# Query projection of a fused cross-attention kernel: by batch, or turned for teams of three batches

## Chip, cores, metric

One core of a Trainium2 chip. The time is device microseconds of one execution. The kernel is one launch with five engines (PE for products, DVE, ACT, POOL, and SP, which here only issues DMAs), each with its own instruction list in a fixed order; they meet by semaphores.

## What is computed

For each of 16 batches (100 query rows, 361 context rows, width 512, float32): grouped-query attention with 32 query heads, 8 key/value heads of width 16, an output projection with residual and layer norm, and then a second, single-headed cross-attention with residual. Cut to what matters:

```
q = x @ Wq + bq;  k = c @ Wk + bk;  v = c @ Wv + bv
scores = einsum('bkgld,bksd->bkgls', q, k) / sqrt(16) + mask
attn = softmax(scores);  out = einsum('bkgls,bksd->bkgld', attn, v)
x = layernorm(out @ Wo + bo + x) * gamma + beta
s = (x @ w_q.T) @ (c @ w_k.T).T / sqrt(512)
x = x + alpha * ((softmax(s) @ (c @ w_v.T)) @ w_o.T)
```

## The kernel before

Precision is kept by splitting a float32 operand into a high and a low part (`_h`, `_l`); `product` (L707 to L711) then runs three matmuls for one. All four lists are written out by hand, call by call: batch b's `heads`, batch b-1's `scores` and `values`, and batch b-2's later stages are interleaved in pieces on PE.

- Query projection, per batch b: `x_turned_in` loads x transposed (xT, one buffer); ACT `x_high` and POOL `x_low` split it; PE `q_part` runs 4 x 3 matmuls with x as the weights (100 columns) and Wq moving (512 columns) into `work` bank 1; DVE `q_natural` adds the bias (`row_n`); PE `turn_q` transposes in four pieces; ACT `q_high` and DVE `q_low` split, with the scale 0.25; SP `queries_out` writes both parts to DRAM (`q_dr`) in two DMAs. `k_part` and `v_part` (Wk, Wv as 128-column weights, context moving, 362 columns) and `turn_v` use the same bank.
- `stacks_in` reads keys and queries back as stacked operands `ks`, `qs`. PE `heads` (L750) computes each head's scores in natural layout only for the row maximum, which DVE `maxima` takes (L2372). `turn_maxima`, `maxima_high`, `maxima_low` turn and split 16 maxima for each half of the heads; SP `maxima_in` (L246) copies them as two more rows into `qs`. `scores` waits for both (`m_in`), once for each half.
- `scores` (L730, L737, L738) computes transposed scores minus maximum; DVE and ACT move them to SBUF, POOL and DVE add the mask, ACT takes exp. `values` (L766) multiplies with V and a ones column; the rest (`y_part`, `xm_part`, `s1_part`, `cx_part`, `d_part`, L823 and L874) finishes layer norm and the second attention.
- At the start, `fold_m` (L883) and `fold_n` (L897) multiply pairs of second-layer weights once; weights are split by `high_part` and `low_part`; POOL clears and sets rows of `ks` and `qs` (`zero_rows`, `one_rows`).

Of the kernel before, what the change touches and what calls it, by code (L numbers as in the profile page):

```python
# [5 lines left out]
F32 = mybir.dt.float32  # L6
# [8 lines left out]
P = 128  # L15
# [4 lines left out]
JL = J * L  # L20
END = B - 1
# [20 lines left out]

def ring(b, par, dmas=1):

    return (8 * b - 8 * par + 16) * dmas


def build(nc, xT_d, x_d, ctxT_d, ctx_d, mask_d, maskT_d, wq_d, wk_d, wv_d, wo_d, bq_d, bk_d, bv_d,
          bo_d, gamma_d, beta_d, w1q_d, w1k_d, w1v_d, w1o_d, alpha_d, out_d):
    with ExitStack() as ctx:  # L50
# [19 lines left out]
        bq_b, gamma_b, beta_b, bo_b = (sb(n, [L, H]) for n in ("bq_b", "gamma_b", "beta_b", "bo_b"))  # L70
        bk_c, bv_c = sb("bk_c", [P, 1]), sb("bv_c", [P, 1])
# [7 lines left out]
        x_h, x_l = sb("x_h", [P, JL], F32R), sb("x_l", [P, JL], F32R)  # L79
        c_h, c_l = sb("c_h", [P, KT * SP2], F32R), sb("c_l", [P, KT * SP2], F32R)  # L80
        row_n = sb("row_n", [L, H])
        q_h, q_l = sb("q_h", [P, JL], F32R), sb("q_l", [P, JL], F32R)
# [9 lines left out]
        mt_h = [sb(f"mt_h{h}", [NH // 2, L], F32R) for h in range(2)]  # L92
        mt_l = [sb(f"mt_l{h}", [NH // 2, L], F32R) for h in range(2)]
# [26 lines left out]

        def turned_of(b):
            return r_b if b == END else turned

        def parts(b):
            return (x_h, x_l) if b == END else (u_h, u_l)


        k_dr = nc.dram_tensor("k_dr", (2, 2, HD, KVH, SC * P), F32, kind="Internal").ap()
        q_dr = nc.dram_tensor("q_dr", (2, 2, HD, KVH, JL), F32, kind="Internal").ap()
# [13 lines left out]
        q_mm, q_nat, q_tr, qh_ok, ql_ok = (sem(n) for n in ("q_mm", "q_nat", "q_tr", "qh_ok", "ql_ok"))  # L143
# [30 lines left out]
        def _(sp):  # L174
# [11 lines left out]
            def biases():  # L186
                sp.dma_start(bk_c[:, :], bk_d).then_inc(w_b, 16)
                sp.dma_start(bv_c[:, :], bv_d).then_inc(w_b, 16)
                sp.dma_start(bq_b[:, :], bq_d).then_inc(w_b, 16)
# [15 lines left out]
            def fold_n_in(k):  # L205
                if k == 0:
                    sp.wait_ge(wh_ok["q"], 1)
                    sp.wait_ge(wl_ok["q"], 1)
# [16 lines left out]
            def stacks_in(b, half, r0, r1):  # L225
                p = b % 2
                if r0 == 0:
                    wait(sp, q_out, 32 * (b + 1))
# [4 lines left out]
                for r in range(r0, r1):  # L233
# [3 lines left out]
                             q_dr[p, :, :, gs, :].rearrange("r d g c -> (r d) g c")).then_inc(st_in[half][p], 16)  # L237

            def maxima_in(b, half):
# [3 lines left out]
                for row, t in ((TERMS, mt_h[half]), (TERMS + 1, mt_l[half])):  # L243
# [70 lines left out]
            def queries_out(b):  # L314
                p = b % 2
                wait(sp, qh_ok, b + 1)
                wait(sp, ql_ok, b + 1)
                wait(sp, st_in[0][p], 96 * (b // 2))
                wait(sp, st_in[1][p], 96 * (b // 2))
                sp.dma_start(q_dr[p, 0, :, :, :].rearrange("d g c -> g d c"), q_h[:, :].bitcast(F32)).then_inc(q_out, 16)  # L320
                sp.dma_start(q_dr[p, 1, :, :, :].rearrange("d g c -> g d c"), q_l[:, :].bitcast(F32)).then_inc(q_out, 16)
# [17 lines left out]

            weights_q()  # L340
            x_turned_in(0)
            ctx_turned_in(0)
            fold_m_in(0)
            weights_k()
            biases()
            weights_o()
            weights_v()
            fold_m_in(1)
            fold_n_in(0)
            fold_n_in(1)  # L350
            x_turned_in(1)
            queries_out(0)
            keys_out(0)
# [4 lines left out]
            ctx_turned_in(1)  # L358
            stacks_in(0, 1, 0, 2)
            queries_out(1)  # L360
            mask_turned_in(0)
            stacks_in(0, 1, 2, 4)
            mask_in(1)
            fold_m_in(3)
            x_turned_in(2)
# [4 lines left out]
            stacks_in(1, 0, 2, 4)  # L370
            x_turned_in(3)
            norm_in()
            ctx_in(0)
            residual_in(0)
            maxima_in(0, 1)
            stacks_in(1, 1, 0, 2)
            stacks_in(1, 1, 2, 4)
            queries_out(2)
            ctx_turned_in(3)
            mask_turned_in(1)  # L380
            keys_out(2)
            mask_in(2)
            rows_out(0, 0)
            maxima_in(1, 0)
            stacks_in(2, 0, 0, 2)
            stacks_in(2, 0, 2, 4)
            rows_out(0, 1)
            stacks_in(2, 1, 0, 2)
            sums_in(0)
            rows_in(0)  # L390
            maxima_in(1, 1)
            x_turned_in(4)
            reciprocals_out(0)
            stacks_in(2, 1, 2, 4)
            reciprocals_in(0)
            queries_out(3)
            ctx_turned_in(4)
            keys_out(3)
            maxima_in(2, 0)
            mask_in(3)  # L400
            mask_turned_in(2)
            rows_out(1, 0)
            stacks_in(3, 0, 0, 2)
            stacks_in(3, 0, 2, 4)
            late_keys_in(0)
            rows_out(1, 1)
            stacks_in(3, 1, 0, 2)
            mask_turned_in(3)
            sums_in(1)
            maxima_in(2, 1)  # L410
            stacks_in(3, 1, 2, 4)
            rows_in(1)
            x_turned_in(5)
            reciprocals_out(1)
            late_keys_in(1)
            reciprocals_in(1)
            residual_in(1)
            rows_out(2, 0)
            ctx_in(1)
            mask_in(4)  # L420
            queries_out(4)
            maxima_in(3, 0)
            keys_out(4)
            stacks_in(4, 0, 0, 2)
            stacks_in(4, 0, 2, 4)
            stacks_in(4, 1, 0, 2)
            rows_out(2, 1)
            maxima_in(3, 1)
            result_out(0)
            ctx_turned_in(5)  # L430
            residual_in(2)
            sums_in(2)
# [3 lines left out]
            x_turned_in(6)  # L436
            mask_turned_in(4)
            reciprocals_in(2)
            rows_out(3, 0)
            ctx_turned_in(6)  # L440
            queries_out(5)
            mask_in(5)
# [3824 lines left out]
```

## Time and profile before

| | us |
|---|---|
| median of 3 runs | 670.9 (666.88 to 673.54) |
| the profiled execution | 673.24 |
| its span, first to last instruction | 671.5 |
| PE busy in the span | 637.4 |
| DVE, POOL, ACT busy | 494.7, 398.4, 395.9 |
| mean granted TensorE clock | 0.992 |

The span is what all views divide; the execution's own time is 1.74 us longer. A matmul's listed duration includes its way through the array, which overlaps with the next one, so what a matmul costs is the distance between two starts.

### The profile page before, as it was taken

Reading aid. Unit: us, or ns where it says so; the run is one execution under the profiler, and the core shown is the slowest. Engines: PE = TensorE matmul, PEld = TensorE weight load, DVE = VectorE, ACT = ScalarE, POOL = GpSimd, SP = SyncE. Lnnn points to the kernel's source line nnn. Section 1 sums busy time; section 2 is a strip of 40 time slices with the busy share of each in tenths; the row PEclk is TensorE's granted clock in tenths of the full one; section 3 lists DMA queues with packets and bytes.
Section 4 is the critical chain, followed back from the end, with each engine's and each line's share of the span. In section 5 each row is a group of like instructions: output and inputs, shape, how many; then the busy total and the mean of one; then the engine's idle time right before and its main releaser. Section 6 shows DMA issues by size and latency. Waiting matters only on the chain.

```text
span 671.5 us, 11779 instructions
## 1 busy us (share of the span) xinstructions
PE 637.4 (95%) x3720; PEld 467.3 (70%) x3720; DVE 494.7 (74%) x1453; ACT 395.9 (59%) x588; POOL 398.4 (59%) x254
## 2 busy tenths in 40 slices
PE   3989889999999999999999999999999999999887
PEld 2646557777767878777777778787777777766454
DVE  2258678877688787878787887878787888885742
ACT  3314576666657666666656576666667666666321
POOL 7243758756475766667665657666676666563220
PEclk9999888999999999999999999999999999999999
DMA  8687755755574766757475757667675755534212
GB/s 287 217 180 206 163 158 140 195 162 139 141 252 111 223 164 190 165 174 208 132 214 120 232 119 225 161 194 165 183 194 145 197 143 149 120 98 137 88 45 71
DMA packets 47354, 110.93 MB, mean 165 GB/s; under 512 B 10094, under 2 KB 31662, under 8 KB 46782
## 3 DMA queue, kind: packets, MB, share of 16 engines
q1 hardware_dynamic: 47294, 110.19, 60.0%
q8 instruction: 30, 0.49, 0.3%
q14 instruction: 30, 0.25, 0.1%
HBM read 87.29 MB, written 22.46 MB: 163 GB/s over the span
## 4 chain that ended last, share of the span: by engine, by line
PE 74%; DMA 9%; POOL 5%; issue 5%; DVE 2%; SPq 2%; ACT 2%; POOLq 0%; DVEq 0%; ACTq 0%
PE mx_ps L750 11%; PE work L709 10%; PE work L710 10%; PE work L711 10%; PE o_ps L766 8%; PE work L823 5%; PE work L874 5%; PE sc_ps L737 3%; DMA qs<-mt_l 3%; PE sc_ps L730 3%; PE sc_ps L738 3%; PE work L779 3%; POOL pr L3914 3%; DMA late<-r_dr 2%; DMA k_dr<-k_l 1%
## 5 line engine op out<-in xcount | busy, mean ns | idle before, releaser
L2372 DVE CUSTOM_DVE_ANT_0 mx_ps<-mx_ps,mask_n 100x361 f32<-100x361 f32 x512 | 271.4, 542 | 68.5 <-PE mx_ps L750 63.6
L3914 POOL TENSOR_TENSOR pr<-pr,mask_t 128x800 f32<-128x800 f32 x124 | 236.8, 1917 | 72.2 <-ACT pr L3218 69.8
L750 PE MATMUL mx_ps<-ks,qs 96*100 96x362 f32 x512 | 182.2, 370 | 3.3 <-DMA qs<-q_dr 2.3
L3225 ACT ACTIVATE pr<-pr 128x1200 f32<-128x1200 f32 x128 | 149.3, 1206 | 9.5 <-POOL pr L3914 5.6
L3218 ACT ACTIVATE pr<-sc_ps 128x800 f32<-128x800 f32 x124 | 104.0, 839 | 76.4 <-PE o_ps L766 50.3
L750 PEld LDWEIGHTS mx_ps<-ks,qs 96*100 96x100 f32 x512 | 84.4, 166 | 40.4 <-DVE mx L2372 12.2
L2358 DVE TENSOR_TENSOR pr<-sc_ps,mask_t 128x400 f32<-128x400 f32 x124 | 70.8, 571 | 26.0 <-PE sc_ps L730 14.4
L3926 POOL TENSOR_TENSOR c_l<-cT,c_h 128x1448 fp32r<-128x1448 f32 x16 | 53.3, 3330 | 55.1 <-ACT c_h L3250 55.1
L766 PE MATMUL o_ps<-pr,va 128*32 128x400 f32 (+1 forms) x768 | 73.9, 519 | 0.0
L2372 DVE DVE_READ_ACCUMULATOR2_ANT mx<- 100x1 f32 x512 | 72.0, 141 | 0.0
L823 PEld LDWEIGHTS work<-late 128*128 128x128 f32 (+1 forms) x384 | 49.7, 191 | 7.0 <-issue 5.9
L730 PE MATMUL sc_ps<-qs,ks 98*128 98x400 f32 x128 | 48.8, 381 | 4.2 <-DMA qs<-mt_l 4.0
L823 PE MATMUL work<-late 128*128 128x100 f32 (+1 forms) x384 | 52.2, 274 | 0.0
L874 PE MATMUL work<-late 128*100 128x362 f32 x128 | 49.1, 472 | 0.7 <-ACT late L3281 0.7
L737 PE MATMUL sc_ps<-qs,ks 98*128 98x400 f32 x128 | 47.0, 367 | 2.8 <-DMA qs<-mt_l 2.3
L766 PEld LDWEIGHTS o_ps<-pr,va 128*32 128x32 f32 (+1 forms) x768 | 22.3, 112 | 34.6 <-issue 32.2
L738 PE MATMUL sc_ps<-qs,ks 98*128 98x400 f32 x128 | 44.4, 347 | 0.0
L709 PE MATMUL work<-wq_h,x_h 128*100 128x512 f32 x64 | 30.5, 476 | 10.9 <-POOL x_l L3920 10.9
L3920 POOL TENSOR_TENSOR x_l<-xT,x_h 128x400 fp32r<-128x400 f32 x16 | 18.4, 1149 | 28.9 <-ACT x_h L3244 28.9
L730 PEld LDWEIGHTS sc_ps<-qs,ks 98*128 98x128 f32 x128 | 24.3, 190 | 12.2 <-DMA qs<-mt_l 4.7
L737 PEld LDWEIGHTS sc_ps<-qs,ks 98*128 98x128 f32 x128 | 24.4, 191 | 8.4 <-DMA qs<-mt_l 3.1
L3931 POOL TENSOR_SCALAR ve<-mv 100x1 f32<-100x1 f32 x16 | 7.5, 467 | 36.9 <-DVE mv L2453 36.9
(157 smaller groups left out, 1207.1 us busy)
## 6 DMA issues: line engine op xcount, KB each, us to landing
qs<-q_dr SPq DMA_DIRECT2D x64, 200.0 KB, 4.3
ks<-k_dr SPq DMA_DIRECT2D x128, 96.0 KB, 3.7
late<-in_ctx SPq DMA_DIRECT2D x16, 768.0 KB, 7.3
cT<-in_ctxT SPq DMA_DIRECT2D x16, 724.0 KB, 5.5
late<-in_ctxT SPq DMA_DIRECT2D x16, 724.0 KB, 6.0
o_dr<-o_s SPq DMA_DIRECT2D x30, 200.0 KB, 3.9
xT<-in_xT SPq DMA_DIRECT2D x16, 200.0 KB, 3.9
q_dr<-q_h SPq DMA_DIRECT2D x16, 200.0 KB
```

Of the source, the lines that this page charges most:

```text
L709: nc.tensor.matmul(dst, lh, rh, start=(k == 0), stop=False)
L730: nc.tensor.matmul(sc_ps[:, 0, 0:JL], ks[p][:, g, 0:P], qs[p][:, g, :], start=True, stop=True).then_inc(s0_mm, 1)
L737: nc.tensor.matmul(sc_ps[:, 1, 0:JL], ks[p][:, g, P:2 * P], qs[p][:, g, :], start=True, stop=True)
L750: nc.tensor.matmul(mx_ps[0:L, n % 2, 0:SP2], qs[p][0:TERMS, g, L * j:L * (j + 1)], ks[p][0:TERMS, g, 0:SP2], start=True, stop=True).then_i ...
L766: mm = nc.tensor.matmul(o_ps[32 * q:32 * (q + 1), 0:JL], va[p][0:k, c, 4 * half + q, :], pr[0:k, q, c, :], start=(c == 0), stop=(c == SC - 1))
L823: mm = nc.tensor.matmul(work[:, late_bank(b), L * t:L * (t + 1)], ctx_n[0:k, c, P * t:P * (t + 1)], p1_t[0:k, c, :], start=(c == 0), stop= ...
L874: mm = nc.tensor.matmul(work[0:L, late_bank(b), 0:SP2], turned_of(b)[:, L * k:L * (k + 1)], cT_s[:, SP2 * k:SP2 * (k + 1)], start=(k == 0) ...
L2358: V.tensor_tensor(pr[:, g % 4, 0, :].rearrange("p (j l) -> p j l", j=J), sc_ps[:, 0, 0:JL].rearrange("p (j l) -> p j l", j=J), mask_t[p][: ...
L2372: V.tensor_tensor_reduce(out=src, in0=src, in1=mask_n[p][:, :], scale=1.0, scalar=-3.0e38, op0=ALU.add, op1=ALU.max, accum_out=mx[p][:, n: ...
L3218: A.activation(pr[:, g % 4, 1:3, :], sc_ps[:, 1:3, 0:JL], ACT.Copy).then_inc(sc_cp, 1)
L3225: A.activation(t, t, ACT.Exp).then_inc(ex_ok, 1)
L3914: G.tensor_tensor(t, t, mask_t[p][:, 1:3, :].unsqueeze(2).to_broadcast([P, 2, J, L]), ALU.add).then_inc(sc_pool, 1)
```

## The change

From batch 4 on, queries are projected for three batches at once (batches 4 to 6, 7 to 9, 10 to 12, 13 to 15), and turned: Wq is the weights (128 columns, one of four blocks j), and x of three batches moves (300 columns). The result comes out transposed, so bias and split are one ACT and one DVE instruction for each j, and `q_natural` and `turn_q` go for these batches. The results go to DRAM by `team_out`: six DMAs for each j, of runs of 100 elements (400 bytes), where `queries_out` has two DMAs for each batch with runs of 400 elements. The scale 0.25 is folded into Wq and the bias.

Batch 0's projection is ordered by terms: products with the high halves first, by halves of Wq, whose split is now done in two pieces. Matmuls whose result nobody reads are put into PE's list: 24 of 128x128 float32 before the first product, and 49 of 512 columns in the first batches: 5 before the first heads (`fill_first`), 19 in four groups right ahead of a batch's scores (`fill_scores`, three of them in batches 0 and 1, one in batch 4), and 25 in fifteen groups of 1 to 4 among the heads (`keep_busy`, each behind a wait on DVE's or ACT's reading of the bank that it writes). `mt_h` and `mt_l` become one pair of tiles for both halves, so a half's `maxima_high` waits until the other half's DMAs have landed. All five lists are reordered; x is the first load, `keys_out(0)` moves ahead of `x_turned_in(1)` and `queries_out(0)`, and POOL's `x_low(0)` and `c_low(0)` move ahead of `zero_rows(0)`.

```
+ALONE = 4
+TEAMS = ((4, 3), (7, 3), (10, 3), (13, 3))
+def sent(t, j):
+    return 32 * (ALONE + J * sum(n for _, n in TEAMS[:t]) + (j * TEAMS[t][1] if j else 0))
...
+            def team_out(t, j):
+                b0, n = TEAMS[t]
+                wait(sp, qh_ok, ALONE + J * t + j + 1)
+                wait(sp, ql_ok, ALONE + J * t + j + 1)
+                for k in range(n):
+                    for r, src in ((0, q_h), (1, q_l)):
+                        sp.dma_start(q_dr[b0 + k, r, :, :, j, :].rearrange("d g l -> g d l"),
+                                     src[:, L * k:L * (k + 1)].bitcast(F32)).then_inc(q_out, 16)
...
+            def team_part(t, j, k0, k1):
+                b0, n = TEAMS[t]
+                js = slice(P * j, P * (j + 1))
+                if j == 0 and k0 == 0:
+                    pe.wait_ge(xh_ok, b0 + n)
+                    pe.wait_ge(xl_ok, b0 + n)
+                if k0 == 0:
+                    bank(1, ql_ok, ALONE + J * t + j + 1)
+                for k in range(k0, k1):
+                    mm = product(work[:, 1, 0:n * L], wq_h[:, k, js], wq_l[:, k, js], xs_h[:, k, 0:n, :],
+                                 xs_l[:, k, 0:n, :], k, KT - 1)
...
+            def fill_scores(b, g, c, count):
+                pe.wait_ge(*((sc_add, 8 * b + g) if c == 0 else (sc_cp, 8 * b + g)))
+                for _ in range(count):
+                    nc.tensor.matmul(sc_ps[0:L, 2 if c else 0, :], wk_h[:, 0, 0:L], wq_h[:, 0, :], start=True, stop=True)
...
+            def keep_busy(count, free, value):
+                pe.wait_ge(free, value)
+                dst = sc_ps[0:L, 2, :] if free is fl_ok and value == 3 else o_ps[0:L, :]
+                for _ in range(count):
+                    nc.tensor.matmul(dst, wk_h[:, 0, 0:L], wq_h[:, 0, :], start=True, stop=True)
...
+            warm_up(24)
+            fold_m(3, 0, 1)
             q_part(0, 0, 4)
+            fold_m(1, 0, 1)
+            turn_q(0)
...
             def maxima_low(b, half):
                 dve.wait_ge(mh_ok[half], b + 1)
-                wait(dve, m_in[half], 32 * b)
+                wait(dve, m_in[1 - half], 32 * (b + half))
...
+            def team_low(t, j):
+                n = TEAMS[t][1] * L
+                dve.wait_ge(qh_ok, ALONE + J * t + j + 1)
+                dve.wait_ge(q_out, sent(t, j))
+                V.scalar_tensor_tensor(q_l[:, 0:n], work[:, 1, 0:n], bq_c[:, j:j + 1], q_h[:, 0:n].bitcast(F32),
+                                       ALU.add, ALU.subtract).then_inc(ql_ok, 1)
...
+            def team_high(t, j):
+                n = TEAMS[t][1] * L
...
+                act.wait_ge(q_mm, ALONE + J * t + j + 1)
+                act.wait_ge(q_out, sent(t, j))
+                A.activation(q_h[:, 0:n], work[:, 1, 0:n], ACT.Identity, bias=bq_c[:, j:j + 1]).then_inc(qh_ok, 1)
...
             constants()
-            zero_rows(0)
             x_low(0)
             c_low(0)
+            settle(cl_ok, 1)
+            zero_rows(0)
```

## Rows read from the trace of the kernel before

**Rows 1.** The page's part 1: busy us (share of the span) x instructions.
```profile
PE 637.4 (95%) x3720; PEld 467.3 (70%) x3720; DVE 494.7 (74%) x1453; ACT 395.9 (59%) x588; POOL 398.4 (59%) x254
```
**Rows 2.** Busy time of each engine in stretches: one middle batch, and the end.
```profile
272.49:309.25 36.76, 36.76 (x232) 28.36 (x236) 29.66 (x90) 24.30 (x36) 24.16 (x15) 1.00 0.66 177
...
600.00:640.00 40.00, 35.79 (x209) 21.53 (x202) 28.25 (x58) 19.07 (x29) 14.59 (x13) 1.00 0.33 108
640.00:671.50 31.50, 24.70 (x130) 16.50 (x128) 8.80 (x18) 6.29 (x17) 3.39 (x5) 0.99 0.20 62
```
**Rows 3.** The same view of early stretches: us, PE, PEld, DVE, ACT, POOL, clock, DMA, GB/s.
```profile
0.00:10.87 10.87, 0.00 (x1) 0.03 (x1) 2.29 (x2) 3.62 (x3) 8.97 (x11) 1.00 0.74 256
10.87:19.30 8.43, 8.34 (x23) 4.96 (x24) 1.96 (x3) 3.59 (x4) 3.32 (x1) 1.00 0.95 357
...
67.00:117.00 50.00, 44.11 (x237) 29.75 (x236) 36.64 (x123) 31.96 (x45) 34.76 (x19) 0.90 0.60 154
...
78.00:82.00 4.00, 4.00 (x28) 1.32 (x27) 1.57 (x5) 0.70 (x2) 0.17 (x1) 0.67 0.23 51
```
**Rows 4.** PE's instructions in order of time, in one middle batch.
```profile
286.38 0.39 PE L709 MATMUL work<-wq_h,x_h 128*100 128x512 f32 x1
286.61 0.40 PE L710 MATMUL work<-wq_l,x_h 128*100 128x512 f32 x1
...
293.47 0.39 PE L750 MATMUL mx_ps<-ks,qs 96*100 96x362 f32 x1
293.70 0.51 PE L779 MATMUL work<-ident,row_n 100*128 100x100 f32 x4
294.04 0.83 PE L823 MATMUL work<-late 128*128 128x100 f32 x6
...
296.88 0.33 PE L709 MATMUL work<-c_h,wk_h 128*128 128x362 f32 x1
297.05 0.33 PE L710 MATMUL work<-c_l,wk_h 128*128 128x362 f32 x1
```
**Rows 5.** The chain that ended last, in order of time, first 42 us: start, us, what.
```profile
0.73 4.89 DMA late<-in_wq
...
5.65 1.91 ACT wq_h L3185
...
8.14 2.64 POOL x_l L3920
...
12.44 0.43 PE work L709
...
19.98 2.30 DVE wo_l L2338
...
25.36 7.94 DMA k_dr<-k_l
...
35.58 5.57 DMA qs<-q_dr
```
**Rows 6.** The waits of PE: us in total, times, longest us.
```profile
PE sc_ps L730 <- DMA qs<-mt_l: 4.0, 2, 2.8
...
PE sc_ps L737 <- DMA qs<-mt_l: 2.3, 3, 1.4
```
**Rows 7.** A maxima DMA and the scores behind it, in order of time.
```profile
304.13 0.59 SPq L246 DMA_DIRECT2D qs<-mt_l  x1
...
308.22 0.35 PE L737 MATMUL sc_ps<-qs,ks 98*128 98x400 f32 x1
```
**Rows 8.** DMA issues by line: times, KB each, median us to landing.
```profile
qs<-mt_l SPq DMA_DIRECT2D x32, 6.2 KB, 2.4
```
**Rows 9.** L320's issues: SP's ns for one, min/median/max.
```profile
L320 SPq DMA_DIRECT2D q_dr<-q_h x16: 594/620/715, 23.3 to 555.3; - x16
```
**Rows 10.** The page's part 3: packets, MB, share of 16 engines' time.
```profile
q1 hardware_dynamic: 47294, 110.19, 60.0%
```
**Rows 11.** Groups of DVE instructions by line and shape.
```profile
L2401 DVE TENSOR_TENSOR row_n<-work,bq_b 100x512 f32<-100x512 f32 x16 | 11.0, 687 | 6.5 <-PE work L711 6.4
```

More of the change, by code:

```diff
@@ L91, in build @@
         mx = [sb(f"mx{p}", [L, NH]) for p in range(2)]
-        mt_h = [sb(f"mt_h{h}", [NH // 2, L], F32R) for h in range(2)]
-        mt_l = [sb(f"mt_l{h}", [NH // 2, L], F32R) for h in range(2)]
+        mt_h = sb("mt_h", [NH // 2, L], F32R)
+        mt_l = sb("mt_l", [NH // 2, L], F32R)
         mask_t = [sb(f"mask_t{p}", [P, SC, L]) for p in range(2)]
@@ L242, in maxima_in @@
                 wait(sp, ml_ok[half], b + 1)
-                for row, t in ((TERMS, mt_h[half]), (TERMS + 1, mt_l[half])):
+                for row, t in ((TERMS, mt_h), (TERMS + 1, mt_l)):
                     dst = qs[p][row:row + 1, 4 * half:4 * half + 4, :].bitcast(F32).rearrange(
@@ L771, in turn_maxima @@
                 p = b % 2
+                if b == 0 and half == 0:
+                    pe.wait_ge(zero_ok, 2)
                 pe.wait_ge(a_mx, NH * b + 16 * (half + 1))
@@ L951, in pack_rows, with fill_first @@
                                  start=(half == 0), stop=(half == 1)).then_inc(g_mm2[half], 1)
+            def fill_scores(b, g, c, count):
+                pe.wait_ge(*((sc_add, 8 * b + g) if c == 0 else (sc_cp, 8 * b + g)))
+                for _ in range(count):
+                    nc.tensor.matmul(sc_ps[0:L, 2 if c else 0, :], wk_h[:, 0, 0:L], wq_h[:, 0, :], start=True, stop=True)
+            def fill_first(count):
+                for _ in range(count):
+                    nc.tensor.matmul(mx_ps[0:L, 1, :], wk_h[:, 0, 0:L], wq_h[:, 0, :], start=True, stop=True)
@@ L1096, in _ @@
+            q_part(3, 3, 4)
+            heads(2, 3, 5)
+            fill_scores(1, 4, 1, 3)
             scores(1, 4, 1, 3)
             turn_q(3)
+            scores(1, 4, 0, 1)
+            heads(2, 5, 6)
+            values(1, 0)
+            heads(2, 6, 8)
+            k_part(3, 0, 1)
+            heads(2, 8, 9)
+            scores(1, 5, 1, 3)
             heads(2, 9, 10)
-            values(1, 0)
+            k_part(3, 1, 2)
             heads(2, 10, 12)
-            scores(1, 4, 0, 1)
-            k_part(3, 0, 1)
@@ L1436, in _ @@
+            scores(5, 4, 1, 3)
+            k_part(7, 0, 1)
+            heads(6, 12, 13)
             cx_part(3, 0, 1)
-            heads(6, 9, 10)
-            turn_q(7)
+            heads(6, 13, 14)
+            scores(5, 4, 0, 1)
             cx_part(3, 1, 2)
-            heads(6, 10, 11)
+            heads(6, 14, 15)
+            k_part(7, 1, 2)
+            scores(5, 5, 1, 3)
             cx_part(3, 2, 3)
-            heads(6, 11, 12)
+            scores(5, 5, 0, 1)
+            heads(6, 15, 16)
@@ L1693, in _ @@
-            q_part(10, 3, 4)
-            heads(9, 7, 9)
+            turn_v(9)
+            values(8, 0)
+            heads(9, 7, 8)
             turn_p1(6)
-            values(8, 0)
+            heads(9, 8, 9)
+            team_part(2, 3, 0, 1)
+            scores(8, 4, 0, 1)
+            heads(9, 9, 10)
+            scores(8, 4, 1, 3)
             cx_part(6, 0, 1)
-            heads(9, 9, 10)
-            turn_q(10)
+            heads(9, 10, 11)
             cx_part(6, 1, 2)
-            heads(9, 10, 11)
+            heads(9, 11, 12)
@@ L3088, in _ @@
             centre(12)
+            maxima(14, 22, 23)
             shift(12)
@@ L4011, in _ @@
             add_mask(3, 0)
-            x_low(5)
             add_mask(3, 1)
+            x_low(8)
+            c_low(5)
             add_mask(3, 2)
@@ L4131, in _ @@
             add_mask(11, 0)
-            x_low(13)
+            c_low(13)
             add_mask(11, 1)
```

2999 lines of the change are left out of this document (1499 added, 1500 removed).

## The prediction

> **What bounds the kernel now.** I read the page's shares first. PE is busy 95% of the span, the next engine 74% [rows 1], which leaves 671.5 - 637.4 = 34.1 us in which PE does nothing. That average hides stages, so the second view is the busy time by stretches. In a middle batch, which lasts 36.76 us, PE is busy for all of it, DVE for 29.66, ACT 24.30, POOL 24.16 [rows 2]: there a microsecond off PE is a microsecond off the time, until DVE becomes the limit. The last 71.5 us are different: PE is idle for 4.2 us up to 640 and for 6.8 after it [rows 2]. At the start PE waits 10.87 us for its first operands. Then it runs slowly: from 10.87 to 19.30 the starts of 512-column products stand 0.43 us apart [rows 5], against 0.23 later [rows 4], although the page prints a granted clock of 1.00 there [rows 3]; 0.43 us for 512 columns is 1.2 GHz, 0.23 is near 2.4. Between 67 and 117 us the mean granted clock is 0.90 and PE busy 44.11 of 50 [rows 3]. The waits of PE show what stops it: scores waiting for maxima DMAs, 4.0 and 2.3 us in five waits [rows 6]. The third view is the chain at the start [rows 5]: load of Wq, its split, POOL's x_l (2.64 us), slow products, then the split of Wo (which SP waits for before it may issue more), the keys' way to DRAM (7.94 us), the stacks' way back (5.57 us), and heads at 41.3.
>
> **Teams (batches 4 to 15).** I price a matmul by the distance of starts. With 512 columns it is 0.23 us, with 128-column weights and 362 columns 297.05 - 296.88 = 0.17 (0.165 over several) [rows 4]. Removed per batch: 12 x 0.23 = 2.76 us. `turn_q` holds PE from 293.70 to 294.04, and the head ahead of it takes 0.23 in place of 0.17 [rows 4]: 0.40 us together. That is 3.16 us. Added per team: 4 x 4 x 3 = 48 matmuls of 300 columns with 128-column weights, 16 per batch. No row has that form. The line through the two prices is (0.230 - 0.165)/150 = 0.43 ns a column, so 300 columns cost 0.165 - 62 x 0.00043 = 0.138; I take 0.141 for a slightly larger fixed part. From above it is bounded by 0.165, if weights of 128 columns can't follow each other faster than in those rows; from below by 300 columns at 2.4 GHz, 0.125. So 16 x 0.141 = 2.26 us (2.00 to 2.64). Gain 3.16 - 2.26 = 0.90 us a batch, 12 batches: **10.8 us** (6.2 to 13.9). PE must be the limit for all of this to be seen. A team lays 6.8 us on one batch and a half, and batches without a team have 36.8 - 3.2 = 33.6 us of PE work. DVE there loses `q_natural`, 0.69 us [rows 11], and its share of q_l, and is at some 28.4 us, 85% of 33.6: it still fits. The stage that falls short is the end: the removed `q_part(14)` and `q_part(15)` lie before 600 us, where PE is nearly full, so I count them whole, with 6.2 as the lower end for what late chains may eat. ACT gives one copy for four shorter ones in three batches, in its 12 us of slack a batch [rows 2]: nothing. If that cover is gone, it is the bank that comes free later, a few tenths for each j.
>
> **The start.** Products no longer wait for the whole split of Wq and for POOL. Wq lands at 5.62, and its whole high part takes 1.91 [rows 5]; with x loaded first I put it 0.6 later, the first half of the high part at 7.2, both low halves (DVE) at 9.6. `x_low(0)`, which ran 2.64 us at 8.14 [rows 5], comes before that. The eight late products then run 9.6 to 11.5 at the fast clock, if the warming products have brought it, where the twelve ran from 10.87 to about 10.87 + 12 x 0.43 = 16.0: 4.5 us earlier. The keys of batch 0 wait for `c_low(0)`, then for PE, then for SP, which first waits for the split of Wo (ends 22.28 [rows 5]). With the earlier PE work and `keys_out(0)` ahead of two other issues, I put k_dr's issue near 20 in place of 25.36: 5 us. Its landing (7.94 us) and the stacks' (5.57) [rows 5] contain a backlog of weight loads which the change doesn't shrink, so between 2 and 8 us arrive at the heads. I take **5.5**. The 24 warming products cost nothing while no operand is there; at 0.43 us each they would last 10.3 us from about 1.5, at 0.23 half of that. If the clock rises late, they end after the operands have come and cost up to 1 to 2 us, which is in the lower bound.
>
> **The fills and the clock (41 to 130 us).** In rows, 50 us at a mean of 0.90 [rows 3] are 10 us at the lower level, and lose 5 us of PE's work; the worst stretch, 78 to 82, is at 0.67 with PE busy all of it [rows 3], right after the stall on the maxima. The 49 fills are 49 x 0.23 = 11.3 us of PE. The idle time that they could lie in is 50 - 44.1 = 5.9 us in this stretch, with about 3 more in the 26 us before and 1.4 at batch 4 [rows 6]. They cost 11.3 - 10.3 = 1 us net and give back up to 5: **3.5 us** gained with the reordering (6 gained to 2 lost). A rule of the Trainium skill bears on it ("TensorE: Matmul & The Clock Gate", Part 1): the slow clock is the default and activity releases it. By that, fills that cover each stall give the whole 5 us, 1.5 more than I take; the trace agrees that the fall comes behind a stall, but at 78 to 82 it persists over busy time.
>
> **SP and the DMAs.** `team_out` makes 24 DMAs a team, 96 in all, for 24 of `queries_out`, at 0.62 us of SP each [rows 9]: 44.6 us more of SP, in packs of six (3.7 us). What they can delay is `maxima_in`. In rows, a maxima DMA issued at 304.13 lands after 2.4 us [rows 8] at 306.5 and scores start at 308.22 [rows 7]: 1.7 us of slack. Single tiles `mt_h`/`mt_l` add a wait of ACT and DVE for the other half's landing; halves are some 16 us apart and a landing takes 2.4, so nothing, and behind a late landing DVE's maxima and with them PE would queue. Packets: 256 of 1600 bytes a batch become 1024 of 400. A mean packet takes 0.600 x 16 x 671.5/47294 = 0.136 us of one engine [rows 10]; at that price 768 more are 6.5 us of all sixteen engines a batch, 18 points on a share of 0.66 [rows 2]; by bytes alone they are nothing. I take 1 us lost in all (0 to 6). The Trainium skill ("DMA: Bandwidth & Descriptors", Specifications) says that pieces under 512 bytes are done by read-modify-write and fall below line rate. No row shows such a transfer's rate by itself. [...]
>
> **The sum.** 10.8 + 5.5 + 3.5 - 1.0 = 18.8 us. Span 671.5 - 18.8 = 652.7; own time 673.24 - 18.8 = 654.4. The median shown is 670.9, 2.3 below the profiled execution; scaled by 654.4/673.24 = 0.972 it becomes **652**.
>
> **Rivals.**
> 1. *Another limit takes over.* In batches without a team DVE's maxima, PE's heads and two banks of mx_ps alternate; at 85% DVE the waits between them could keep half of the teams' gain, and the fills only pay for themselves. 5.4 + 5.5 - 1 = 9.9 us: 661. For it: late in the kernel the chain runs through POOL and DMAs; against it: PE has no idle time at all in a middle batch with DVE at 81%.
> 2. *Slower: SP's queue.* Each pack of six ahead of a maxima pair delays scores by 3.7 - 1.7 = 2.0 us. If all 16 packs do, 32 us are lost: 652 + 31 = 683. It turns the sign from about ten packs on; slower landings of small writes add to it (a landing 2 us longer than the slack in 12 batches is 24 us). Against it: SP spends much of a batch waiting, and the packs stand between other issues.
> 3. *The fills don't do what they are for*: the stalls lie elsewhere in the new order, the clock falls all the same, and 49 fills cost their 11.3 us. 10.8 + 5.5 - 11.3 - 1 = 4 us: 667.
> 4. *Weights of 128 columns bound the teams' products* at 0.165: 4.6 us less gain, 657.
> 5. *More*: stalls on maxima (6.3 us [rows 6]) also vanish with the new order, 647.
>
> **Chances and range.** Forecast 0.55, rival 1 0.16, rival 2 0.06, rival 3 0.06, rival 4 0.07, rival 5 0.10. The time is the forecast's. The bounds of its terms reach from about 643 to 663; I set 641 to 664, which takes in rivals 1, 4 and 5 and leaves out 2 and 3. A change below 1% (6.7 us) can hardly be told from none here. Faster than 664 by all cases but 2 and 3 and the tail of 1: 0.87; within 1%: 0.08; slower: 0.05.
>
> **What would show it.** Right: products of 300 columns whose starts stand 0.14 apart; three middle batches together 2.7 us shorter (107.6 for 110.3), one longer and two shorter, with PE still full; first heads near 36; granted clock 1.00 from 60 to 120; no wait of scores on maxima above 2 us. Wrong: PE idle behind DVE's mx reads in batches without a team; scores waiting for qs<-mt_l after a pack of `team_out`; the clock below 1 with fills in place; heads starting at 40 because k_dr lands as late as before.

## The result, and the profile after

The changed kernel takes 678.74 us (median of 4 runs, 677.54 to 680.38); the kernel before took 672.22 beside it. The ratio is 1.0111, 95% interval 1.0063 to 1.0158: 1.1% slower, where I had forecast 2.8% faster. Its profiled execution took 677.62 us, span 675.8. My sum led to a span of 652.7, so 23 us have to be found.

The page after, parts 1 and 3, beside [rows 1] and [rows 10]:
```profile
PE 646.4 (96%) x3817; PEld 478.6 (71%) x3817; DVE 498.8 (74%) x1447; ACT 394.5 (58%) x593; POOL 395.5 (59%) x254
...
q1 hardware_dynamic: 57230, 110.19, 60.0%
```
PE is busy 9 us longer: the teams take work off it, but the 24 warming products and the 49 fills put 7.9 and 13.9 us on (start to start in the trace). 9,936 more packets took no larger share of the DMA engines than before, so the smaller packets that I had worried about show no cost here. Busy time by itself doesn't show where the time is lost.

The busy time by stretches of the kernel after (columns as in [rows 3]): the early stretch; the twelve batches from the first values of batch 3 to those of batch 15; then one stall and what came behind it.
```profile
60.00:130.00 70.00, 65.67 (x377) 45.22 (x377) 57.62 (x176) 43.97 (x60) 45.71 (x28) 1.00 0.63 169
186.55:619.13 432.58, 422.34 (x2617) 323.63 (x2616) 344.92 (x1035) 280.00 (x417) 276.59 (x173) 0.99 0.62 165
276.00:283.10 7.10, 5.36 (x40) 2.97 (x38) 6.23 (x12) 2.98 (x4) 3.77 (x4) 1.00 0.75 171
283.11:289.94 6.83, 5.81 (x19) 5.00 (x20) 4.49 (x12) 3.39 (x6) 2.31 (x2) 0.50 0.21 62
```
The same two long stretches of the kernel before:
```profile
60.00:130.00 70.00, 63.82 (x345) 43.64 (x344) 55.09 (x179) 45.38 (x62) 47.19 (x28) 0.93 0.65 165
181.34:613.91 432.57, 428.73 (x2643) 325.65 (x2643) 349.03 (x1051) 284.39 (x420) 284.70 (x177) 1.00 0.63 170
```
The twelve batches last 432.58 us for 432.57. In that stretch lie the 120 products of ten removed queries and eleven `turn_q` before (10 x 2.76 + 11 x 0.40 = 32.0 us by my prices; 34.4 from start to start in the trace), and the 144 of three teams after (20.3 by price, 21.2 in the trace). PE should have lost 12 to 13 us. It lost 6.4 of busy time, for five fills lie there too (1.1 us) and 10.2 us of the stretch run at the half clock, which makes up to 5.1 us more of busy time; the kernel before has no half clock there. Its idle time rose from 3.84 to 10.24. Ahead of the stretch 5.2 us of the span were lost, behind it 0.9 gained. Ahead of it, the other fills take 12.8 us and the warming products 7.9; PE's idle time there is 10.3 us less (20.4 to 10.1), and the 10.2 us of half clock that the kernel before has there are gone, up to 5.1 us back. 12.8 + 7.9 - 10.3 - 5.1 leaves 5.3, about what is lost.

The products themselves cost what I said. PE's timeline after, a team's product:
```profile
235.61 0.30 PE L737 MATMUL work<-x_h,wq_h 128*128 128x300 f32 x1
235.75 0.31 PE L738 MATMUL work<-x_l,wq_h 128*128 128x300 f32 x1
235.89 0.30 PE L739 MATMUL work<-x_h,wq_l 128*128 128x300 f32 x1
```
Their starts stand 0.14 us apart. What happens nowhere to DVE in the kernel before is this, in the timeline of POOL, DVE and PE (in brackets the idle time before and its releaser; `shift` is L2570, `x_low` L4006, `add_mask` L3992):
```profile
279.56 1.13 POOL L4024 TENSOR_TENSOR rstd<-ve,half_c 100x1 f32<-100x1 f32 x1
280.66 1.04 POOL L4006 TENSOR_TENSOR x_l<-xT,x_h 128x400 fp32r<-128x400 f32 x1
280.77 3.30 DVE L2570 SCALAR_TENSOR_TENSOR x<-y,rstd,beta_b 100x512 f32<-100x512 f32 x1 [0.51 <-DVE y L2558]
281.66 1.86 POOL L3992 TENSOR_TENSOR pr<-pr,mask_t 128x800 f32<-128x800 f32 x1
284.00 0.53 DVE L2463 CUSTOM_DVE_ANT_0 mx_ps<-mx_ps,mask_n 100x361 f32<-100x361 f32 x1
284.13 0.93 PE L809 MATMUL work<-ident,x 100*128 100x100 f32 x4 [2.77 <-DVE x L2570]
```
`shift` takes 0.75 us at its median. Here it starts 0.11 us behind POOL's `x_low`, stands still through it and through the `add_mask` that follows, and ends 0.55 after POOL has. PE waits 2.77 us for it, and from 283.11, a microsecond before PE goes on, the granted clock is 0.50 for 6.83 us (1.2 GHz), as the last of the four stretches shows. The same happens to a tiny operation, the scaling of `bq_c`, that the change brings:
```profile
99.31 3.34 POOL L4013 TENSOR_TENSOR c_l<-cT,c_h 128x1448 fp32r<-128x1448 f32 x1
99.36 3.32 DVE L2493 TENSOR_SCALAR bq_c<-bq_c 128x4 f32<-128x4 f32 x1
102.59 0.67 DVE L2494 SCALAR_TENSOR_TENSOR x<-x,work 100x512 f32<-100x512 f32 x1
```
PE's `turn_q(3)` waits 2.60 us behind it. And to two of the copies in `pick_rows`, at 587 us:
```profile
587.38 3.89 POOL L3992 TENSOR_TENSOR pr<-pr,mask_t 128x800 f32<-128x800 f32 x2 [5.11 <-ACT pr L3275]
587.39 1.92 DVE L2581 COPY cT<-ident 128x64 f32<-128x64 f32 x1
589.24 0.18 DVE L2583 COPY cT<-ident 128x64 f32<-128x64 f32 x1
589.44 1.88 DVE L2583 COPY cT<-ident 128x64 f32<-128x64 f32 x1
```
In the kernel before, no `shift` and no copy was held: POOL was idle when each of them started. The opposite case stood there, though, in the row from which I took 2.64 us for `x_low(0)` [rows 5]:
```profile
7.60 2.29 DVE L2319 TENSOR_TENSOR wq_l<-late,wq_h 128x2048 fp32r<-128x2048 f32 x1 [7.60 <-issue]
8.14 2.63 POOL L3920 TENSOR_TENSOR x_l<-xT,x_h 128x400 fp32r<-128x400 f32 x1 [0.79 <-ACT x_h L3244]
```
The other 128x400 `x_low` of that kernel take 1.03 to 1.06 us. This one starts while DVE splits Wq and ends 0.88 us after DVE has: there POOL was the one that stood still. The waits of PE after show the sum, beside [rows 6]:
```profile
PE work L809 <- DVE x L2570: 4.9, 7, 2.8
PE mx_ps L778 <- DVE mx L2463: 4.4, 5, 2.8
PE work L809 <- DVE x L2494: 2.6, 1, 2.6
```
The waits for the maxima's DMAs, once the largest, are 0.6 us in two. So two of my signs of being right came true (no such wait above 2 us, clock 1.00 from 60 to 130) while the time got longer. One other new wait is of the team's own chain: ACT's `q_h` waits 7.0 us in 6 for the landing of the j before it, while that j's successor holds bank 1 of `work`.

### The profile page after: what moved, and what is told of

Same layout as the page of the kernel before. It is cut to its first block, busy times and chain, and to the rows that moved or that the text cites. A ratio compares the mean times of both kernels' runs of the same rounds, so it can differ in the third digit from the quotient of the medians.

```text
span 675.8 us, 12018 instructions
## 1 busy us (share of the span) xinstructions
PE 646.4 (96%) x3817; PEld 478.6 (71%) x3817; DVE 498.8 (74%) x1447; ACT 394.5 (58%) x593; POOL 395.5 (59%) x254
## 4 chain that ended last, share of the span: by engine, by line
PE 67%; DMA 9%; issue 8%; SPq 5%; DVE 5%; POOL 4%; ACT 2%; POOLq 0%; ACTq 0%; DVEq 0%
PE mx_ps L778 10%; PE work L737 8%; PE work L739 8%; PE work L738 8%; PE o_ps L794 7%; PE work L899 5%; PE work L950 5%; PE sc_ps L765 3%; SPq L344 3%; DMA late<-r_dr 3%; PE sc_ps L758 3%; PE sc_ps L766 3%; PE work L809 2%; POOL pr L3992 2%; DMA q_dr<-q_l 2%
## 5 line engine op out<-in xcount | busy, mean ns | idle before, releaser
L3992 POOL TENSOR_TENSOR pr<-pr,mask_t 128x800 f32<-128x800 f32 x124 | 236.0, 1911 | 116.7 <-ACT pr L3275 115.8
L794 PE MATMUL o_ps<-pr,va 128*32 128x400 f32 (+1 forms) x768 | 71.2, 503 | 0.0
L899 PE MATMUL work<-late 128*128 128x100 f32 (+1 forms) x384 | 50.8, 272 | 0.7 <-ACT late L3360 0.7
L4018 POOL TENSOR_SCALAR ve<-mv 100x1 f32<-100x1 f32 x16 | 9.1, 571 | 40.9 <-DVE mv L2552 40.9
L4029 POOL TENSOR_TENSOR late<-late 128x400 f32<-128x400 f32 x15 | 15.8, 1055 | 25.0 <-DMA late<-r_dr 15.9
L3315 ACT ACTIVATE c_h<-cT 128x1448 fp32r<-128x1448 f32 x16 | 22.5, 1406 | 8.1 <-DMA cT<-in_ctxT 7.6
```

The costliest lines, as they stand in the source:

```text
L794: mm = nc.tensor.matmul(o_ps[32 * q:32 * (q + 1), 0:JL], va[p][0:k, c, 4 * half + q, :], pr[0:k, q, c, :], start=(c == 0), stop=(c == SC - 1))
L899: mm = nc.tensor.matmul(work[:, late_bank(b), L * t:L * (t + 1)], ctx_n[0:k, c, P * t:P * (t + 1)], p1_t[0:k, c, :], start=(c == 0), stop= ...
L3992: G.tensor_tensor(t, t, mask_t[p][:, 1:3, :].unsqueeze(2).to_broadcast([P, 2, J, L]), ALU.add).then_inc(sc_pool, 1)
```

## The experiments

Four theories: V, DVE's operations on SBUF stand still beside POOL; S, six DMAs per j are too much for SP or for the team's chain; F, the 49 fills cost more than they give; O, the new order on all queues is bad as such. All numbers are medians with the ratio to the kernel before, which was run on the same chip each time (670.3 to 671.7 us), and its 95% interval. A point is a hundredth of the ratio, 6.7 us.

**1. No fills.** `keep_busy`, `fill_scores` and `fill_first` calls removed.

> The changed kernel without its 49 fills (the 24 warming products ahead of the first operands stay). Theory F, the fills cost more than they give: their starts hold PE for 13.9 us of the changed kernel's account, and they give back at most the slow clock of 77 to 105 us in the kernel before (three stretches of 3.4 us at half speed, 5 us of PE's work). Without them 4 to 9 us less: 670 to 675 for 678.7. Rival: they stand only where PE would wait anyway, so taking them out only turns them into waits and brings the slow clock back: 678 to 684.

673.49 us, ratio 1.0037 (0.9994 to 1.0081): 0.74 points, 5.0 us, less than the change. F holds in the change as it stands. But the `shift` that lasted 3.30 us at 281 lasts 1.42 here, and the half clock of 6.83 us at 283 is gone. By the starts of the batches' first maxima 2.0 of the 5.6 us between the two spans come from batch 6 to batch 7, where that `shift` stands. So a part of the 5.0 us may be V's.

**2. Two DMAs per j.**
```
-for k in range(n):
-    for r, src in ((0, q_h), (1, q_l)):
-        sp.dma_start(q_dr[b0 + k, r, :, :, j, :].rearrange("d g l -> g d l"), ...)
+for r, src in ((0, q_h), (1, q_l)):
+    sp.dma_start(q_dr[b0:b0 + n, r, :, :, j, :].rearrange("b d g l -> (d g) b l"), ...)
```


> The changed kernel, but each j of a team is sent with two DMAs in place of six (same bytes and same 400-byte pieces; the columns of Wq and bq are laid out by dimension and then head, so that one DMA reaches all 128 rows of three batches). SP loses 64 issues of 0.6 us, 38 us in all, and the team's next high part can start 2.4 us earlier. Theory S, SP's queue and the chain high, low, DMAs, landing, next high hold bank 1 of work and with it PE: 4 to 8 us less, 671 to 675. Rival: SP has room and bank 1 is not what is waited for: within 2 us of 678.7.

668.65 us, 0.9964 (0.9941 to 0.9986): 9.9 us less, more than S said. The edit also lays out Wq's columns by dimension and then head, and sends the single queries of batches 0 to 3 by the same merged rows. Here too the `shift` near 280 lasts 1.43 us for 3.30 and the half clock behind it is gone: 5.5 of the 9.8 us between the two spans come from batch 6 to batch 7. With DVE held, this run doesn't separate S from V; run 10 does.

**3. DVE free of POOL.**
```
-if b == ALONE - 1: V.tensor_scalar(bq_c, bq_c, 0.25, ...)      # in q_natural
+if b == 0: ...
 x_low(11); variance(4); deviation(4); settle(x1_ok, 5)         # same for 7; settle after deviation(3)
```


> The changed kernel with four operations moved and nothing else: the scaling of bq_c goes from the fourth query to the first; x_low(11) and x_low(14) go on POOL ahead of variance and deviation; POOL waits for the end of shift after deviation(3), (4) and (7). Theory V, DVE's operation on two SBUF tensors stands still while POOL computes (shift 3.30 us at 280.8, 1.80 at 242.5 and 1.46 at 393.3 for 0.75, the scaling of bq_c 3.32 us for a tiny tensor), PE stands behind it and the clock falls (6.8 us at half speed from 283.1): 5 to 9 us less, 670 to 674, no shift above 0.8 us at those places, no slow clock at 283. Rival: these stalls are made up by later slack, or others take their place: 676 to 679.

671.3 us, 1.0017 (0.9986 to 1.0049): 6.3 us less. No shift is held, the clock at 283 us stays full. The copies of `pick_rows`, which the edit leaves alone, still were (1.92 and 1.88 us). But the scaling, moved to the first query, met `c_low(0)` there and was held again:
```profile
L2493 DVE TENSOR_SCALAR bq_c<-bq_c x1: 2247/2247/2247, 12.8 to 12.8; 128x4 f32<-128x4 f32 x1
```
and the first heads came at 42.41 us for 39.40. That is V once more, at a place where I hadn't meant to try it.

**4. Teams in the old order.** The five lists of the kernel before, with team calls in place of those of the single queries.

> The kernel before's own order on all five queues, with the teams alone put in: no fills, no warming products, no products by terms at the start; the four j of a team are spread, one in the batch two ahead of the team, two in the next and one in the team's own first (team 0: all four in batch 4), in the places where the single queries stood and between the keys' and values' products. Six DMAs per j as in the change. Theory O, the teams' arithmetic is worth what it was priced at (10.8 us) and the change's own order eats it: 672.2 less 8 to 12, 660 to 664. Rival: teams give nothing once their x, high and low parts and DMAs are paid on ACT, DVE, POOL and SP, whatever the order: 670 to 675.

745.04 us, 1.1095: far worse than either theory. Its waits of PE:
```profile
PE work L737 <- DVE q_l L2504: 24.7, 9, 7.0
...
PE work L984 <- ACT xm_n L3391: 7.9, 5, 2.9
PE work L737 <- POOL x_l L4045: 7.5, 3, 3.0
```
This was my layout, not the teams: products of the next user of bank 1 stood directly behind a team's, and the x of teams 1 to 3 came too late (the last line, at 229, 353 and 480 us). It says nothing for or against O, except that a place in the order costs more than the arithmetic saves.

**5 and 6. All three causes out; the same with the fills kept.** The edits of 1, 2 and 3, the scaling now on ACT, and on POOL:
```
 deviation(b)
+settle(x1_ok, b + 1)      # for b < 14
...
+settle(pick_ok, 5)
 add_mask(14, 4)
```


> The changed kernel with three causes taken out together: no fills; two DMAs per j; DVE kept from POOL: the scaling of bq_c on ACT, POOL waits for the end of shift after every deviation and for the four copies of pick_rows before add_mask(14, 4). If the three causes are separate, their parts add up: alone they gave 5.2, 10.1 and 7.4 us, so 678.7 - 22.7 = 656 (654 to 660), ratio to before 0.977. If they are one and the same chain (each of the three merely shortens the same late chain), the sum is not reached: 664 to 668.

> The same as the run with all three causes taken out, but the 49 fills are kept. It tells what the fills are worth when the other stalls are gone. Theory F: they still cost, 5 us more than without them (661 for 656), though the clock holds at 1.00 up to 580. Rival: with the other stalls gone the clock that they hold is worth more than they take: 652 to 656.

Without fills 655.65 us, 0.9767 (0.9691 to 0.9844); with them 657.9, 0.9808 (0.9724 to 0.9892). The first lies on the sum of the three differences. Whether fills still cost, 0.4 points, is inside the intervals. The stretches of the run without fills:
```profile
60.00:130.00 70.00, 63.10 (x356) 42.01 (x356) 56.68 (x182) 45.70 (x64) 47.45 (x28) 0.98 0.67 184
180.51:598.45 417.94, 415.17 (x2613) 319.61 (x2612) 337.03 (x1035) 279.61 (x417) 277.59 (x173) 1.00 0.63 171
```
The twelve batches take 417.94 us for 432.57, 14.6 less: 13.6 of PE's busy time, where the prices give 11.7 and the products' starts 13.3, and 1.1 of idle time. The order of the change, with its three faults out, lets all of the teams' gain through: O falls.

**7. The start alone,** in the kernel before.

> The kernel before with the change's start alone, up to the first heads (x ahead of Wq, Wq split in halves, the first query's products by terms, 24 warming products, the keys' way out ahead of x_1 and the queries), and from there its own order; queries of all batches one by one. If the start is worth what its first heads show in the changed kernel (39.4 for 41.3), 1 to 3 us less than before: ratio 0.996 to 0.999. My prediction said 5.5: ratio 0.992.

671.34 us, 1.0004 (0.9958 to 1.005). The first heads start at 38.72 for 41.28, 2.6 us earlier, and no gain can be measured in the time. The interval of 3 us either way still holds the 1 to 3 us that I expected, but not the 5.5 of the prediction. Its one profiled execution was 5.0 us shorter than that of the kernel before (span 666.5); the ten runs reach from 667.95 to 677.0. The run also has the change's single pair of `mt_h` and `mt_l`.

**8. Teams in the old order, second layout.**

> Teams alone in the kernel before's order, second layout: two DMAs per j, two j of a team in the batch ahead of its first and two in its first, both between the values of the batch ahead and the keys (in the first layout the values stood directly behind a team's product and waited 2.2 us for bank 1 each time, and keys' low parts held it 2.4 us before). No fills, no start changes, the scaling of bq_c on ACT. Theory O: teams pay when nothing waits for them: 671.3 less 6 to 10, 661 to 665. Rival: the team chain (product, high, low, DMAs, landing, next high) doesn't fit into any order with single q_h and q_l without stalls of PE: 672 or more.

704.95 us, 1.0494 (1.0426 to 1.0562). PE's waits above a microsecond behind the first heads are 7 with 20.0 us for 19 with 49.5 in run 4, yet four middle batches take
```profile
235.62:391.61 155.99, 148.45 (x922) 113.92 (x921) 116.61 (x356) 97.07 (x145) 93.99 (x59) 0.99 0.63 167
```
39.0 us each, against 36.8 before. In the whole kernel PE waits for DVE's maxima 24.2 us in 53 waits at the weight loads (12.2 in 37 before) and 5.9 in 11 at the heads (0.8 in 3). I read it so: the removed products had stood between the heads, and without them two heads follow each other faster than DVE reads them, so teams need heads laid anew. No run tries that by itself. And 18 of the 31 us by which the span is longer come from batch 3 to batch 4, where team 0's 6.8 us of products stand and waits of 5.37 and 3.95 us for `q_l`, at 153 and 164 us. I could not show the teams in an order of my own.

**9 to 12. Each cause put back, and the old start.** 9: DVE held as in the change; 10: six DMAs; 11: two DMAs and four tiny ones that nobody waits for; 12: start of the kernel before.

> The run with all three causes taken out, but DVE is again held by POOL as in the changed kernel (no waits of POOL for shift and pick_rows, the scaling of bq_c on DVE beside c_low). So no fills, two DMAs per j. If theory V's part is what it was alone (0.9 points of the ratio, 6.3 us), and the parts are separate: 655.7 + 6.3 = 662, ratio 0.986. If it was only the accident of one stall at 281 us that two DMAs already avoid: 656 to 658, ratio under 0.980.

> The run with all three causes taken out, but six DMAs per j as in the changed kernel (and Wq's columns in its layout). Theory S: SP's queue is late and with it the team's next high part: 655.7 + 9.9 = 665.5, ratio 0.991. Rival: without the other stalls SP has room for them: 656 to 659.

> The run with all three causes taken out, and behind the two DMAs of each j four more that nobody waits for (128 pieces of 4 bytes each, to a DRAM tensor that isn't read). SP issues as many as with six DMAs, 64 more in all, but the data of a j is on its way after two. If SP's own time is what six DMAs cost: 4 us or more above 655.7, ratio 0.983 or more. If it is the landing, for which the next high part and bank 1 wait: within 2 us of 655.7, ratio 0.975 to 0.980.

> The run with all three causes taken out, with the start of the kernel before up to the first heads (no warming products, Wq first, the first query k by k). What is left of the change is the teams and their order. If the start was worth the 0 to 3 us that it gave alone: 656 to 659, and the teams alone give 13 to 15 us against the kernel before, ratio 0.977 to 0.982; I had priced them at 10.8, ratio 0.984.

9 gave 670.5 us, 1.0002 (0.9975 to 1.003): V costs 2.35 points, 15 us, once the fills are gone and two DMAs are sent, not 6. Its shift at 279 us lasts 3.30 us again, and from 60 to 130 its clock is 0.90:
```profile
60.00:130.00 70.00, 60.99 (x310) 38.85 (x312) 52.38 (x167) 42.18 (x57) 44.18 (x25) 0.90 0.62 166
```
By the starts of the first maxima, of the 15.6 us between its span and that of run 5, 3.4 are there at batch 2, with a wait of 2.41 us for maxima at 87 us: their DMA is issued at 81.06 as in run 5 (81.23) and lands later, and no held operation stands before it, so I can't put these 3.4 down to V. 3.2 come by batch 3 (the scaling), 2.7 from batch 6 to 7 (the shift), and 4.7 at `pick_rows`.

10 gave 666.29, 0.9919 (0.9886 to 0.9952), as S said. SP's timeline shows how (one line of each kind):
```profile
246.54 0.58 SPq L344 DMA_DIRECT2D q_dr<-q_h  x1
...
249.61 0.57 SPq L344 DMA_DIRECT2D q_dr<-q_l  x1
250.29 0.73 SPq L279 DMA_DIRECT2D den<-o_dr  x1
...
252.88 0.58 SPq L264 DMA_DIRECT2D qs<-mt_h  x1
253.52 0.57 SPq L264 DMA_DIRECT2D qs<-mt_l  x1
```
DVE had `mt_l` ready at 247.8. Its DMA is issued 5.8 us later, behind a pack of six and what had queued behind that, and lands after 5.9 us for 2.4 at the median. Then, in PE's timeline and the stretch behind it:
```profile
259.49 0.70 PE L765 MATMUL sc_ps<-qs,ks 98*128 98x400 f32 x1 [2.05 <-DMA qs<-mt_l]
```
```profile
259.50:265.90 6.40, 6.40 (x25) 6.38 (x26) 2.28 (x7) 0.84 (x1) 1.87 (x1) 0.50 0.72 211
```
Such a place costs 2 us of wait and 3.4 of half clock (6.83 us at half speed): 5.3 of the 11.2 us between this span and that of run 5 come from batch 6 to 7, where it stands. With two DMAs the same maxima are issued at 245.55 and nothing waits. Another 2.7 are there at batch 2, before any team's DMA, with a wait of 2.02 us for maxima at 86 us: like the one in 9, these are issued on time (80.87) and land late. No shift is held in 10 or in 5, so here six DMAs stand by themselves against two: 10.6 us by medians.

11 gave 746.89, 1.1127 (1.109 to 1.1165), outside both expectations. One idle DMA takes SP 0.45 us at the median, so SP isn't fuller than with six; but what is queued behind their 512 pieces of 4 bytes lands late:
```profile
ACT q_h L3363 <- DMA q_dr<-q_l: 42.0, 8, 12.8
PEld sc_ps L767 <- DMA qs<-mt_l: 17.2, 7, 7.9
```
So it measured the pieces, not SP.

12 gave 656.83, 0.9805 (0.9734 to 0.9875): the teams and their order alone, 13 us faster than before, and the start is worth at most a few (1.2 us by medians, 2.5 by ratios, inside the intervals).

**13 to 16. What was still open.** 13: as 11, but six idle DMAs of one 400-byte piece each. 14: shifts held, all else free. 15: `maxima_in(1, 0)` ahead of `keys_out(2)` and `rows_out(0, 0)` on SP. 16: the scaling of `bq_c` and `pick_rows` held, the shifts free.

> The run with all three causes taken out, and behind the two DMAs of each j six more of a single piece of 400 bytes each, that nobody waits for. At some 0.4 us each they take 2.4 us of SP per j, as the four extra DMAs of the change did (3.4 us for six against 0.87 for two), but bring hardly any packets. If SP's own time is the cost: 3 us or more above 655.7, maxima of batch 5 issued late near 250, ratio 0.982 or more. If not: within 2 us of 655.7.

> The run with all three causes taken out, but POOL no longer waits for the end of shift: the three shifts at 241, 279 and 388 us are held again (1.65, 3.3 and 1.5 us for 0.75), the scaling of bq_c and pick_rows stay free. From the held run's milestones (values of batch 6 to 7: 2.6 us later; the rest lost at 100 and 583 us) it should cost 3 to 4 us: 659, ratio 0.981 to 0.984. If shift is the main part of the 15 us: 664 or more.

> The run with all three causes taken out, and on SP the maxima of batch 1's first half go ahead of the keys of batch 2 and of rows_out(0, 0), behind which they are issued 1.8 us late (ready at 79.6, issued at 80.6 and 81.2, scores wait at 84). If that stall brings the slow clock of 85 to 120 us, the clock stays full there, and the median falls by 1 to 3 us: 653 to 655, ratio 0.973 to 0.976, with less scatter. If the clock falls for another reason: no change.

> The run with all three causes taken out, but the scaling of bq_c is on DVE beside c_low again and pick_rows runs beside add_mask(14, 4) again; POOL still waits for the end of every shift. If these two carry most of the 15 us (each stops PE for 2 to 3 us and may bring the slow clock): 665 to 669, ratio 0.991 to 0.997. If the shift at 279 us, held for 3.3 us, carried it: 658 to 661, ratio 0.982 to 0.986.

13: 658.03 us, 0.9829 (0.977 to 0.9889). The maxima of batch 5 are issued at 247.68, 2.1 us later, and the scores wait 0.8. The time is 2.4 us up by medians and 4 by ratios, the first between the two expectations, and both inside the intervals; its idle packs took 1.9 us where a pack of the change adds 2.5. The trace of 10 shows SP's lateness at work; how the rest divides between it and the landings stays open.

14: 656.99, 0.9809 (0.9753 to 0.9864): by medians the held shifts cost 1.3 us here, less than I said, by ratios 2.8, and neither is clear of the intervals. The one at 271 us lasts only 1.42 us, for `add_mask` hadn't been ready: the shift of 3.30 us, which was to be put back, didn't come back. 16: 666.17, 0.9944 (0.9908 to 0.9979): two small operations cost 10 us, as expected if they carry most of V. In its stretches, `pick_rows` and what follows:
```profile
573.00:579.00 6.00, 3.22 (x26) 3.05 (x26) 5.93 (x11) 1.70 (x3) 3.76 (x2) 1.00 0.64 213
579.05:582.46 3.41, 3.41 (x15) 3.13 (x14) 2.72 (x9) 1.62 (x4) 0.34 (x1) 0.50 0.05 18
```
PE idles 2.8 of 6 us and then runs at half clock for 3.4.

15: 656.4, 0.9815 (0.9762 to 0.9868). The wait at 84 us vanished, the clock still fell once at 90.7, and the time didn't change: that idea fell.

Together, the eight kernels of the three causes, as ratios ("DVE free" at 1.0017 is the narrower edit of run 3, which left the scaling and `pick_rows` held):

| | six DMAs | two DMAs |
|---|---|---|
| DVE held, fills | 1.0111 | 0.9964 |
| DVE held, no fills | 1.0037 | 1.0002 |
| DVE free, fills | 1.0017 | 0.9808 |
| DVE free, no fills | 0.9919 | 0.9767 |

The three effects alone are 0.74, 1.47 and 0.94 points, 3.15 in sum, and all three out give 3.44. In between they don't simply add. With DVE held, six DMAs or two differ by 1.47 points with the fills and by 0.35 without; taking the fills out with two DMAs gained nothing (0.9964 to 1.0002). Two things differ in the traces there: without the fills the clock from 60 to 130 is 0.90 for 1.00, and the shift near 280 lasts 3.30 us again for 1.43. It is that long in the change and in 9, where it meets two operations of POOL, and not in 1, 2 or 14, where it meets one: how the two lists stand to each other at that place changes with every edit.

## Why the prediction was wrong

**Teams, 10.8 us: right** in the price, and near in the sum. 0.14 us per product; 13.3 us from start to start in a stretch where the prices give 11.7; teams with the old start 13 us by medians, which hold the reordering too. No run shows the teams without it: both of my own orders were slower. That PE would have no idle time behind DVE held only once DVE was free.

**"I take 1 us lost in all" for SP: the step that failed most.** I had the issue's price (0.57 us measured, 0.62 taken), the packs of six and the 1.7 us of slack, and wrote the price of a missed maxima as 2.0 us. I then gave it 0.06, because SP spends much of a batch waiting. It took few places: what queues behind a pack goes with it, and the stall brings the half clock behind it. Measured 10.6 us where nothing is held (10 against 5); about half of it is one wait of 2.05 us for maxima behind a pack, at 259 us, with 6.83 us of half clock, and how the rest comes about stays open. In the change itself the price is 9.9 us, but there the waits for maxima are only 0.6 us, and more than half of it lies where the held shift stands, which meets two operations of POOL with six DMAs and one with two. So the mechanism that I had priced and thrown away shows in 10 and not in the change's own trace. The packets, at which I looked instead, show no cost: two DMAs carry the same pieces, and DMAs on `q_dr` land after 4.1 us at the median in the change for 4.3 before.

**Missing altogether: DVE beside POOL.** I priced `q_natural`'s and q_l's loss on DVE and never asked what POOL would be doing when a given DVE operation starts. The reorder changes that pairing for every operation. The Trainium skill ("SBUF — State Buffer", section "SBUF: two separate sides") says that DVE and GpSimd share a pair of ports as an exclusive lock, taken by a DVE operation in a two-port mode, or by one with two SBUF inputs if the GpSimd operation reads SBUF, and that the other "fully blocks". The traces agree for the shift (3.30 us for 0.75), and `memset` held nothing; the scaling and the copies have one SBUF input and were held, but that they ran in a two-port mode no row says. The maxima, whose first operand is in PSUM, run at 0.53 us beside POOL. My own rows had the sign of it, `x_low(0)` at 2.64 us where 1.03 is its time. By that rule I could have listed the operations at risk, and the new one at 99 us could be read off the lists: `c_low(3)` on POOL beside `q_natural(3)` on DVE. Measured 0.94 points by the narrower edit and up to 2.35 by the full one, 6 to 15 us.

**Fills, 3.5 us gained: wrong in sign in the change.** They do hold the clock (1.00 from 60 to 130, for 0.93). But what they took was larger (13.9 us from start to start, 11.3 by my price), and they took little of the idle time: of the 10.3 us that I counted, no row has the 3 from 41 to 67 us, where PE idles 1.3; and from 41 to 130 it idles 8.5 us without fills (1) and 4.3 with them, 2.6 of these behind the held scaling. The clock then fell elsewhere, at 283 and 594 us. 5.0 us lost, a part of them by the moved shift, where 3.5 were gained in the sum. Its mechanism is rival 3's, at a lower price than the full 11.3 us.

**Start, 5.5 us: too much.** First heads 1.9 us earlier (39.40). The keys' low part left SP at 22.88 for 25.36 [rows 5], 2.5 us earlier and not 5, and the way to the stacks kept its length. `wk_l` was held beside `c_low(0)` (2.27 us for 0.69). In the time, nothing could be measured (7) or up to a few us (12).

The terms that the runs found (S 9.9 less the 1 that I had taken, V 6.3, fills 5.0 + 3.5, start some 3.5) make 27 us; the ratio missed by 3.9 points, 26 us. The sizes overlap, so this is a check of the order of size only. The range was too narrow by its own terms: the lower ends of teams, start, fills and SP (6.2 + 2 - 2 - 6) add up to a gain of 0.2 us, a time near 671, where I wrote 663. (Rival 5's 647 should read 646.) The sign failed because the six DMAs and the held DVE, neither of which my range took in, came together with the fills' loss, and the half clock stood behind several of the stalls.

## What to carry to other kernels

A new order is a change by itself. Before pricing what moves on the bottleneck, lay the lists of two engines that share a path side by side, here DVE's SBUF operations against POOL's, and ask of each small operation what runs beside it and what PE does if it takes 3 us. A stall of 1.6 to 3.3 us on PE can cost twice its length: behind 15 of the 20 between 45 and 620 us (without runs 4, 8 and 11) the clock was at half for 3.4 or 6.8 us (1.7 or 3.4 us of work), behind others, as at 103 us in the change and at 282 in 9, not at all. Send what one step produces in as few DMAs as the layout allows: changing the order of Wq's columns made six into two and was worth more than any fill. The version with all three faults out is 2.3% faster than the kernel before (1.6 to 3.1% by its interval).

## What the runs showed of the hardware

DVE's shift, scaling and copies between SBUF tensors, started during a POOL operation between SBUF tensors, stood still until POOL stopped, over two POOL operations where these followed each other at once: 3.30 us for 0.75; 3.32 for the scaling, which takes DVE 0.17 us with POOL idle (run 7); 1.92 for a copy of 0.18. It goes the other way too: `x_low(0)` of the kernel before took POOL 2.63 us for 1.03 behind DVE's split of Wq. `memset` on POOL didn't hold DVE (`wo_l` 2.29 us beside it, as without it before), nor was DVE's reciprocal held (0.76 us with or without POOL).

8,192 pieces of 4 bytes, 32 KB in all, made landings in the same queue up to 13.2 us long and the kernel 91 us slower than without them (11 against 5). Pieces of 400 bytes in place of 1600 showed no such cost: the DMA engines' share stayed at 60.0%.

The kernel before took 665.35 us at a mean granted clock of 1.000 and 675.29 at 0.990, on the same chip beside runs 13 to 15. Which stall brings the half clock differs from one execution to the next, so one profile doesn't settle a term of under 5 us.
